# The loop over six of eight batches, written out on every engine

## The reference

```python
xn = _layernorm(x)
# attention branch, 16 heads of 16
x_proj = silu(xn @ W1 + b1)
u, v, q, k = split(x_proj, 4)
scores = einsum('bqhd,bkhd->bhqk', q, k)
attn = silu(scores) / S
av = einsum('bhqk,bkhd->bqhd', attn, v)
y1 = _layernorm(av * u, gamma, beta) @ W2 + b2
# feed-forward branch, 256 -> 1024 -> 256, ternary weights
h = gelu(layer_norm(xn) @ ternary(w1).T + b1)
y2 = layer_norm(h) @ ternary(w2).T + b2
out = x + y1 + y2
```

## Time and profile before

| | us |
|---|---|
| median of 3 runs | 1596.24 |
| the runs | 1594.32 to 1603.69 |
| the profiled execution | 1597.45 |
| its span, from the first to the last instruction | 1595.7 |

### The profile page before, as it was taken

How to read it: one execution, slowest core, us unless ns; L and a number is a source line. 1 busy time by engine, 2 the same in 40 slices (tenths; PEclk the granted TensorE clock), 3 DMA queues, 4 the chain that set the end, 5 groups by cost and what they waited for, 6 DMA issues and landing times.

```text
span 1595.7 us, 27804 instructions
## 1 busy us (share of the span) xinstructions
PE 1482.5 (93%) x9826; PEld 778.7 (49%) x9826; DVE 896.9 (56%) x1716; ACT 1223.6 (77%) x1285; POOL 98.7 (6%) x193
## 2 busy tenths in 40 slices
PE   4799999999999999999999999999999999999986
PEld 3345455454554454544545455545455445554443
DVE  4466734666366653666546674376734666457543
ACT  2578886888868887788877888678886888868883
POOL 2000100001000100001000010000100010000000
PEclk9799999999999999999999999999999999999998
DMA  6561034510444106421165113451044410543100
GB/s 182 112 132 35 20 85 107 127 54 1 108 118 94 54 14 139 113 54 54 41 134 125 38 37 80 107 132 54 1 96 111 113 54 1 127 110 82 27 1 27
DMA packets 62330, 123.68 MB, mean 78 GB/s; under 512 B 7664, under 2 KB 9328, under 8 KB 61168
## 3 DMA queue, kind: packets, MB, share of 16 engines
q1 hardware_dynamic: 62192, 121.81, 32.4%
HBM read 79.84 MB, written 41.94 MB: 76 GB/s over the span
## 4 chain that ended last, share of the span: by engine, by line
issue 93%; POOLq 6%; POOL 1%; DVE 0%; DVEq 0%
POOLq L517 3%; POOLq L509 1%; POOLq L493 1%; POOL rs L503 1%; POOLq L502 0%; POOLq L511 0%; POOLq L507 0%; POOLq L505 0%; POOLq L519 0%; POOLq L522 0%; POOLq L203 0%; POOL rs L494 0%; DVE part L764 0%; DVEq L203 0%; POOLq L536 0%
## 5 line engine op out<-in xcount | busy, mean ns | idle before, releaser
L550 ACT ACTIVATE attn<-scores 128x1024 f32<-128x1024 f32 x1024 | 983.2, 1025 | 260.6 <-PE scores L920 259.7
L939 PE MATMUL outs<-attn,V 128*32 128x512 f32 x4096 | 501.0, 607 | 0.0
L920 PE MATMUL scores<-QS,KS 64*128 64x512 f32 x2048 | 407.9, 461 | 74.8 <-ACT attn L550 51.9
L920 PEld LDWEIGHTS scores<-QS,KS 64*128 64x128 f32 x2048 | 165.3, 186 | 390.6 <-ACT attn L550 314.6
L939 PEld LDWEIGHTS outs<-attn,V 128*32 128x32 f32 x4096 | 108.0, 110 | 240.8 <-issue 240.7
L793 DVE SCALAR_TENSOR_TENSOR hid<-fill,ratq,fb1b 128x512 f32<-128x512 f32 x128 | 96.2, 751 | 75.3 <-PE fill L994 70.0
L810 DVE TENSOR_TENSOR tmp<-fill,l2g 128x512 f32<-128x512 f32 x128 | 88.5, 692 | 88.8 <-PE fill L1003 77.5
L1010 PE MATMUL fill<-Wq,hgh 128*128 128x256 f32 x512 | 130.6, 293 | 0.0
L976 PE MATMUL fill<-xp,W1h 128*128 128x512 f32 x384 | 125.5, 408 | 2.3 <-DVE xp L834 1.5
L1010 PE MATMUL fill<-Wq,hgl 128*128 128x256 f32 x512 | 124.9, 282 | 0.0
L1010 PEld LDWEIGHTS fill<-Wq,hgh 128*128 128x128 f32 x512 | 97.3, 190 | 18.0 <-issue 10.4
(11 more groups left out here) (110 smaller groups left out, 1415.1 us busy)
## 6 DMA issues: line engine op xcount, KB each, us to landing
QS<-q_scratch SPq DMA_DIRECT2D x128, 256.0 KB, 7.2
k_scratch<-kst SPq DMA_DIRECT2D x64, 256.0 KB
q_scratch<-qst SPq DMA_DIRECT2D x64, 256.0 KB
KS<-k_scratch SPq DMA_DIRECT2D x64, 256.0 KB, 4.1
KS<-k_scratch SPq DMA_DIRECT2D x128, 128.0 KB, 5.0
xin<-in_x SPq DMA_DIRECT2D x8, 1024.0 KB, 6.2
out_dram<-part SPq DMA_DIRECT2D x16, 512.0 KB, 2.6
w1raw<-in_W SPq DMA_DIRECT2D x1, 1024.0 KB, 7.0
```

Of the source, the lines that this page charges most:

```text
L550: nc.scalar.activation(attn_of(g)[:, 2 * hf:2 * hf + 2, :], SP[:, 2 * hf:2 * hf + 2, :], ACT.Silu).then_inc(s_silu, 1)
L920: ins = mm(SP[:, j, :], KS[rows, pair, t * P:(t + 1) * P], QS[rows, pair - c * PPC, h * HALF:(h + 1) * HALF], start=True, stop=True)
L939: ins = mm(OP[32 * j:32 * j + 32, g // RUN % 2, :], V[:, t, c * HPC // 2 + j, o * DH:o * DH + 2 * DH], attn_of(g)[:, n, :], start=(o == 0 ...
```

## The change

The five hardware loops become Python loops, so that the six batches are written out one behind the other in each engine's program. The order of the work, the slots, the tiles and the semaphores stay as they are. With `b` a Python number, every wait compares with a constant, and the instructions that compute such values in registers and the branches at the end of a batch are gone. The number of instructions in the program grows accordingly.

```diff
@@ -471,7 +471,7 @@
             body(0, first=True)
-            with sp.Fori(1, NB - 1) as b:
+            for b in range(1, NB - 1):
                 body(b)
             body(NB - 1, last=True)
@@ -533,7 +533,7 @@
             body(0, first=True)
-            with pool.Fori(1, NB - 1) as b:
+            for b in range(1, NB - 1):
                 body(b)
             body(NB - 1, last=True)
@@ -623,7 +623,7 @@
             body(0, first=True)
-            with act.Fori(1, NB - 1) as b:
+            for b in range(1, NB - 1):
                 body(b)
             body(NB - 1, last=True)
@@ -886,7 +886,7 @@
             body(0, first=True)
-            with dve.Fori(1, NB - 1) as b:
+            for b in range(1, NB - 1):
                 body(b)
             body(NB - 1, last=True)
@@ -1080,7 +1080,7 @@
             body(0, first=True)
-            with pe.Fori(1, NB - 1) as b:
+            for b in range(1, NB - 1):
                 body(b)
             body(NB - 1, last=True)
```

## The result

| | before | after |
|---|---|---|
| median of 11 runs, us | 1598.38 | 1605.57 |
| lowest and highest, us | 1594.32, 1603.69 | 1602.01, 1607.31 |
| profiled execution, us | 1597.45 | 1605.09 |
| its span, us | 1595.7 | 1603.2 |

A forecast was written before the change was run, and what follows sets the result against it. It took PE, ACT and their semaphores as one chain through all batches. Edges gave -5.8 us and half clocks +7.65, net +1.9: 1599.3 us from the profiled execution, put at 1599.0 us, range 1591 to 1606.

The forecast's parts named there:

- no measurement could tell so small a change: Whole kernel: +0.1 to +0.2% is too small to tell, as a measurement could tell about 1% either way, 16 us.
- The edges were to be 114.6, 116.2 or 117.5 us and nothing else: Between batches: edge lengths follow the granted clock behind the K wait: 1.00, a short 0.50 or a long 0.50.
- no inner part was to grow by over 1 us: First to fourth gelu start of a batch: stays at 74.9 to 75.0 us; growth over 1 us would mean fresh-code stalls.
- Constants for register arithmetic, nothing: Inner parts of batches: register instructions, 24.2 us at PE's L917, are covered by waits, so removing them gains nothing.
- K's transfer takes the branch's place: PE at slot 4: a wait for K's second half replaces the branch stall, leaving 0.4 to 0.5 us per branch.
- The clock: PE behind five new K waits: three short half clocks, a long one and none, adding 7.65 us.
- The edge into batch 1, -0.2 us: Edge from batch 0 to 1: constants on its second side gain 0.35 us at most; 0.2 taken.
- Outside the edges, nothing: Inner parts: nothing taken for them; the profiled execution's 1.75 us beyond the span was left unchanged.
- the whole branch comes back: Rival at PE's loop branches: five at 3.55 us are gained, 17.8 us, giving 1578.5 us; chance 0.03.
- Full clock behind a full K wait: Rival at slot 4: every K wait keeps full clock, only -5.8 us stay, 1590.4 to 1591.7 us; chance 0.12.
- A long half clock everywhere: Rival at slot 4: a long half clock behind every K wait, +8.5 us, 1604.7 to 1605.9 us; chance 0.17.
- Stalls by fresh code in ACT, SP or POOL: Rival in written-out batches: one 3.55 us instruction-supply stall in each of six, +21.3 us, 1617 to 1619 us; chance 0.03.

The follow-up runs named there:

- K first: Pieces of slots 59 and 60 swapped, so K's second half leaves earlier: 1571.29 us (0.9826) in the written-out kernel, 1605.59 us (1.003) in the looped one.
- the products in the gap: Fully written-out kernel plus ten repeated score products on PE before its wait for K's second half at slot 4: 1595.72 us, ratio 0.997.

## Why the prediction was right or wrong

The forecast was 1599.0 us, +0.1 to +0.2%, with 1591 to 1606. The measured change is +0.4%, at 1605.57 us, 0.4 us below the top of the range. From the median then known the forecast was +2.8 us, and +7.2 us was measured. Only 3.8 of the 7.2 us stand at the edges, where the prediction had its terms; the rest it had put at nothing. So the mechanism was right, and that the total fell inside the range is in part luck. The prediction also held that no measurement could tell so small a change; the interval of the 11 runs, 1.0023 to 1.0056, does.

Some of its own signs of being wrong came up. The edges were to be 114.6, 116.2 or 117.5 us and nothing else: 118.4 into batch 3 and 116.8 into batch 7 are neither, since K's transfer was longer there. And no inner part was to grow by over 1 us: batch 0's grew by 1.6 us. That was to speak for fresh code, but batch 0 has the same code in both kernels, and what changed there was the clock.

*Constants for register arithmetic, nothing.* Right. The inner parts of batches 1 to 7 are the same in both kernels, and keeping the loops of SP, POOL and ACT cost nothing with K first.

*K's transfer takes the branch's place.* Right in place, and in size for five of seven batches: 2.3 to 2.6 us had been said for each batch. It was 2.36 to 2.65 in five, but 2.94 in batch 7 and 3.54 in batch 3, where the scores came 17.6 and 18.2 us behind the write and not 17.0 to 17.3. The kernel with PE and DVE written out had 3.43 us in batch 3 as well. Why is open. One detail was wrong: the second half of K is made in slot 60, not in slot 58 as the text said. The chain was measured from SP's write and not from the slot, so that no number changes.

*The clock.* The term that was too small. For the five edges three short half clocks, a long one and none had been taken, 3 x 1.60 + 2.85 = 7.65 us. There were four short ones and a long one: behind the wait in batch 3 the clock was 0.50 for 6.6 us, and it took 15.6 us from slot 4 to slot 8, against 14.5 in the others. At the sum's prices that is 4 x 1.60 + 2.85 = 9.25 us. The longer wait in batch 3 adds about 1.1 us (3.54 against 2.4 to 2.5). The sum for the five edges was -5.6 + 7.65 = +2.05 us; it should have been -5.6 + 9.25 + 1.1 = +4.75 us, and +4.6 us was measured. The 1.60 us and the 114.6 us that go with full clock were right, as the products in the gap showed, and as the edge into batch 1 showed in two other kernels. The prediction had to work this edge out, since its trace held none; those two show it directly.

*The edge into batch 1, -0.2 us.* It came out at -1.4, since before it had had a long half clock and now has a short one. The waits for K were nearly the same, 2.53 and 2.65 us. In other kernels it was 114.7 us (PE alone written out), 114.8 (all but PE) and 116.1 us (PE and DVE). In the first two the clock stayed at 1.00 behind waits of 2.41 and 2.64 us, so a wait of this length does not always bring a half clock. What decides is open.

*Outside the edges, nothing.* The profiled execution has 3.7 us more in the head, batch 0's inner part and the tail (0.2 + 1.6 + 1.9), where the instructions are the same. The clock fell at 170.0 us in batch 0, which it did not before. Other kernels with the same code there had 75.0 as well as 76.6 us, and an inner part of 76.6 us stands once to four times in 8 of the 13 profiled executions, in looped and written-out batches alike. The tail goes from 78.1 to 81.8 us over the 13, and the kernel before has one of the shortest. Over 11 runs the difference of the medians is 7.2 us, of which the edges explain 3.8; these spreads speak for chance in the rest, but whether it has to do with the change is open. The kernel with PE and DVE written out, whose edges are the same, was at 1.0007.

*Of the rivals,* that the whole branch comes back (17.8 us) was wrong here. With K first, PE's branch and DVE's together are worth 1.003 against 0.9826, 2.0%. How it divides is less sure. By the ratios (1.003 with both branches, 0.9924 with PE's alone, 0.9826 with neither) about half is DVE's. By the five edges of the profiled executions (595.5, 571.2 and 560.5 us) DVE's is 24.3 us and PE's 10.7 us, so that PE's branch by itself gave less than the 17.8 us even there. Full clock behind a full K wait occurred in none of batches 1 to 7 of this kernel; it did with the products in the gap, and into batch 1 of two other kernels. A long half clock everywhere did not occur: there was one, in batch 3. Stalls by fresh code in ACT, SP or POOL did not occur.

*What the prediction missed* is DVE. It said that the register instructions of DVE were covered, and took the branch's cost from the rows of branches. ACT's 45 ns were read as "it found its code", which is right for ACT, but DVE's row of 63 ns looks the same and has 4.6 us behind it. In the sum this had no price, since the change removes DVE's stall along with PE's. With PE alone it decides.

The rule weighed in the prediction, from the Trainium skill (Runtime: NRT & Kernel Launch, Instruction fetch mechanics), says that a taken branch out of the fetched code waits for a DMA fetch. The rows of the kernel before agree on a stall for PE, at 3.3 to 3.8 us, and for DVE, at 4.4 to 4.7 us; that a fetch is what is waited for is supported for DVE by q14 above, and is not shown for PE. ACT, SP and POOL go on after 0.1 to 0.2 us. Its conclusion, that writing out is preferred, holds at 2.0% on the order with K first and fails by 0.4% on the given one.

## What to carry to other kernels

A stall that goes away is worth only its lead over the next one that ends at the same place. Look for what else becomes ready there, on every engine and in every queue, and remove them together: alone, writing out the loop cost 0.4% and moving K cost 0.3%, and both together gave 1.7%. A stall at a branch is to be sought in the gap behind the branch's row as well as in the row: PE's stood in the row, DVE's in the gap. And where PE has to wait for some 2.4 us, the price is mostly the wait and a half clock behind it, 1.6 us more.

## What the runs showed of the hardware

- DVE's second gap behind a taken branch, in which it waits for nothing that the profile shows, was longer the earlier the K loads were issued. It was 0.7 to 2.0 us with the loads issued 3.4 to 3.8 us behind the branch (the kernel before, and PE alone written out). With K first it was 3.1 to 3.6 us with the loads 0.7 to 1.2 us ahead of the branch, and 5.5 to 6.4 us in six of seven edges with the loads 1.5 to 1.8 us ahead. The seventh had 2.57 us; what differed there is open. That the gap is a wait for code is inferred from q14.
- Ten unneeded products on PE in front of a wait made the kernel shorter, 0.997 against 1.004, by keeping the granted clock at 1.00 in six of seven edges.
- Standing for 2.4 to 3.5 us was followed by a granted clock of 0.50 in each of batches 1 to 7 of the written-out kernel, but not into batch 1 of two others, after 2.41 and 2.64 us.
- Loads of K issued 1.8 us behind a write of Q, where they had been issued 5.4 us behind it, after it had landed, delayed the landing of that write: ACT's wait for it into batch 1 went from 1.40 to 2.71 us, and the longest of eight from 1.4 to 2.9 us. With those loads back in their place it was 1.4 us again.
